# Mamba block and two attention layers on one core: one order for the whole run per engine, set-up split between engines, silu as one ScalarE function, two more PSUM banks for the last attention tiles

## What is computed

```python
# mamba
u = x @ in_w + in_b
u = silu(conv4(u) + conv_b)                      # causal, 4 taps, per channel
delta = softplus((u @ dt1_w + dt1_b) @ dt2_w + dt2_b)
A_bar = exp(delta[..., None] * A)                # 16 states per channel
h = A_bar * h + Bu                               # a scan over 256 tokens, per state
y = (einsum(h, C) + D_vec * u) * silu(x @ gate_w + gate_b)
x = layernorm(x + y @ out_w + out_b)
# twice, with weights of its own each time
h = shift_token(x);  q, k, v = split(h @ wqkv)   # 8 heads of 64
q, k = rotary(l2norm(q) * qs, l2norm(k) * ksc)
x = x + local_attention(q, k, v) @ wo            # windows of 64, own and previous
h = layernorm(shift_token(x)) * lg + lb
a, g = split(h @ w1 + b1);  x = x + (a * gelu(g)) @ w2 + b2
# end: layernorm(mamba's output + the layers' output)
```

## Time and profile before

| What | us |
|---|---|
| median of 3 runs | 1185.32 |
| lowest and highest of them | 1182.23, 1191.19 |
| the profiled execution | 1198.52 |
| its span, first to last instruction | 1196.7 |

### The profile page before, as it was taken

The page is one execution under the profiler, slowest core; times in us unless marked ns, Lnnn a source line. Parts: engine busy times, 40 slices in busy tenths (PEclk is TensorE's granted clock), DMA queues, the critical chain, the costliest instruction groups (busy, mean ns, idle before and its releaser), DMA issues. The chain is left out here.

```text
span 1196.7 us, 26584 instructions
## 1 busy us (share of the span) xinstructions
PE 981.6 (82%) x10304; PEld 575.6 (48%) x10304; DVE 964.0 (81%) x1758; ACT 815.7 (68%) x1833; POOL 480.4 (40%) x261
## 2 busy tenths in 40 slices
PE   2557778888998999899999989898989788876664
PEld 0013344445564556455555655464646465553452
DVE  6595888899889989999999999999999575624612
ACT  1533874786799689886888698869895657642631
POOL 0002420654356525644454545545455344303401
PEclk9587789899999999999999999999999889978967
DMA  6000000000000010001000010000010001000100
GB/s 211 7 1 14 14 11 14 10 20 15 24 10 19 15 28 15 24 19 29 15 23 15 9 38 24 15 24 15 15 24 6 15 24 24 15 10 4 24 10 10
DMA packets 22001, 25.54 MB, mean 21 GB/s; under 512 B 2614, under 2 KB 13937, under 8 KB 21873
## 3 DMA queue, kind: packets, MB, share of 16 engines
q1 hardware_dynamic: 21873, 23.82, 7.8%
HBM read 9.13 MB, written 2.10 MB: 9 GB/s over the span
## 5 line engine op out<-in xcount | busy, mean ns | idle before, releaser
L505 POOL TENSOR_TENSOR rn<-ssc,expo 128x16 f32<-128x16 f32 x64 | 213.2, 3332 | 399.6 <-DVE ssc L863 389.5
L646 ACT ACTIVATE prob<-BB,nbias,rn 128x128 f32<-128x128 f32 x512 | 226.5, 462 | 99.7 <-DVE nbias L905 98.8
L803 DVE TENSOR_TENSOR_SCAN scan<-du,decay 128x1028 f32<-128x1028 f32 x128 | 288.8, 2288 | 2.4 <-ACT decay L591 1.8
L591 ACT ACTIVATE decay<-delta,negA 128x1024 f32<-128x1024 f32 x128 | 145.0, 1159 | 14.9 <-DVE scan L803 14.3
L999 PE MATMUL Y<-scan,diag 64*64 64x512 f32 x1024 | 143.4, 639 | 13.5 <-DVE scan L803 13.5
L999 PE MATMUL A<-wqkv,hT 128*128 128x512 f32 x256 | 131.2, 637 | 9.6 <-DVE ks L880 8.7
L511 POOL TENSOR_TENSOR kr<-kc,ks 128x512 f32<-128x512 f32 x64 | 115.1, 1798 | 26.5 <-DVE ks L880 24.6
L859 DVE TENSOR_REDUCE ss<-sq 128x16 f32<-128x1024 f32 x64 | 77.5, 1211 | 50.6 <-ACT sq L609 50.5
L900 DVE TENSOR_REDUCE nmax<-BB 128x4 f32<-128x512 f32 x128 | 81.8, 680 | 31.9 <-PE BB L999 31.2
L646 ACT ACTIVATION_READ_ACCUMULATOR prob<-BB,nbias,rn 128x1 f32 x512 | 106.8, 209 | 0.0
L609 ACT ACTIVATE sq<-A 128x512 f32<-128x512 f32 x128 | 72.0, 610 | 31.2 <-PE A L999 31.0
(11 more groups left out here) (146 smaller groups left out, 2014.6 us busy)
## 6 DMA issues: line engine op xcount, KB each, us to landing
v_even<-v_odd SPq DMA_DIRECT2D x96, 128.0 KB, 2.3
xT<-in_xT SPq DMA_DIRECT2D x8, 256.0 KB, 2.7
x<-in_x SPq DMA_DIRECT2D x8, 256.0 KB, 3.8
out<-outb SPq DMA_DIRECT2D x8, 256.0 KB, 2.5
wqkv<-in_wqkv SPq DMA_DIRECT2D x1, 1536.0 KB
w<-in_w SPq DMA_DIRECT2D x1, 682.0 KB
wo<-in_wo SPq DMA_DIRECT2D x1, 512.0 KB
bv<-in_bv SPq DMA_DIRECT2D x1, 328.0 KB
```

The source lines that it names most:

```text
L505: pool.tensor_tensor(rn[:, q % 2, :], ssc[:, :], expo[:, 0:2 * HEADS], ALU.pow).then_inc(rn_sb, 1)
L591: act.activation(decay[:, at % A_RING, :, 1:], delta[:, :, :], ACT.Exp, scale=negA[:, n:n + 1]).then_inc(decay_sb, 1)
L646: ins = act.activation(prob[:, h, :], B[a][:, c * P:(c + 1) * P], ACT.Exp, bias=nbias[:, q % 2, h:h + 1], scale=rn[:, q % 2, h:h + 1], acc ...
L803: dve.tensor_tensor_scan(state, step, a, 0.0, ALU.add, ALU.mult).then_inc(scan_sb, 1)
```

## The change

- Each engine's order is now a written list for the whole run (`PE_ORDER` and so on). Nothing repeats. QUAD and TILE are the same, and in the middle of the run each scan block starts after the same or nearly the same number of tiles as before.
- The first three weight transfers (in_w, pv, gate_w) have a semaphore of their own. PE and ACT wait for it alone at the start. xT comes as rows of one array. DVE convolves group 0 before it makes the coefficients.
- GpSimd makes the small identity, the 34 diagonal matrices and the scaled rotary tables. The mask is made by DVE inside the first `sums`.
- Silu is ACT's Silu function, from the convolution's output to u, and from PSUM to the gate. The two tanh instructions' products on DVE are gone; of DVE's step the difference of neighbouring u stays (`differences`).
- `row_max` multiplies all eight maxima by rn in one instruction; `softmax` waits once for it.
- For tiles 53, 55, 57, 59, 61 and 63 (`LATE`) the banks Y0 and Y1, as a pair `YY`, take BB's place.
- SIZES allows groups of other sizes; all are 2 as before.

The core of the diff:

```diff
-TURNS = GROUPS + 17
...
+LATE = [q for q in range(FIRST[-4], len(TILE)) if q % 2]
...
+def banks_of(step, args):
+    banks = HOLDS.get(step, "")
+    return "Y" if banks == "B" and args[0] in LATE else banks
...
-        Y = [bank(f"Y{i}") for i in range(HALF)]
+        YY = ctx.enter_context(nc.psum_tensor("YY", [P, 2 * TOK], F32))
+        Y = [YY[:, i * TOK:(i + 1) * TOK] for i in range(HALF)]
...
+        def pair(q):
+
+            return YY if q in LATE else BB
...
+            for dst, src in [(in_w[:, :], t["in_w"]), (pv[:, :], t["pv"]), (gate_w[:, :], t["gate_w"])]:
+                sp.dma_start(dst, src).then_inc(w_first, 16)
...
+            pool.wait_ge(coeff_done, 1)
+            for h in range(HALF):
+                for n in range(0, NST + 1):
+                    ins = pool.tensor_scalar(diag[:, h, n, :], ident64[:, :], wsum[:, h, n:n + 1], None, ALU.mult)
+            ins.then_inc(diag_done, 1)
...
-            act.wait_ge(w_mamba, M_W)
-            act.activation(negA[:, :], bv[:, BV["A_log"]:BV["A_log"] + NST], ACT.Exp).then_inc(a_exp, 1)
-            act.wait_ge(setup_done, 1)
+            act.wait_ge(w_first, F_W)
...
+            def silu_u(g):
+                act.wait_ge(conv, HALF * TAPS * (g + 1))
+                if g:
+                    act.wait_ge(y_ps, 2 * HALF * g)
+                    act.wait_ge(du_sb, g)
+                act.activation(u[:, both(g), 1:], hu[:, both(g), :], ACT.Silu).then_inc(u_sb, 1)
...
-            def tanh_u(g):
-                act.wait_ge(conv, HALF * TAPS * (g + 1))
...
-                for a in range(2):
-                    dve.wait_ge(max_sb, 2 * q + a + 1)
-                    dve.tensor_tensor(nbias[:, q % 2, a::2], nmax[:, a::2], rn[:, q % 2, a:HEADS:2],
-                                      ALU.mult).then_inc(nmax_sb, 1)
+                dve.wait_ge(max_sb, 2 * q + 2)
+                dve.tensor_tensor(nbias[:, q % 2, :], nmax[:, q % 2, :], rn[:, q % 2, 0:HEADS], ALU.mult).then_inc(nmax_sb, 1)
...
+            convolve(0, 0)
+            convolve(0, 1)
+            coefficients()
...
-            pe.wait_ge(w_mamba, M_W)
-            pe.wait_ge(setup_done, 1)
-            pe.wait_ge(zeros_ready, 1)
+            pe.wait_ge(w_first, F_W)
...
+                if q == LATE[0]:
+                    pe.wait_ge(m_sum, GROUPS)
```

More of the change, by code:

```diff
@@ L134 @@
[L134 to L137, removed]
-def order(table):
-    for turn in range(TURNS):
-        for step, age, *rest in table:
-            g = turn - age
-            if not 0 <= g < GROUPS:
-                continue
-            if step in TILE_STEPS:
-                yield step, (TILE.index((rest[0], g, rest[1])),) + tuple(rest[2:])
-            elif step in FFN_STEPS:
-                yield step, (QUAD.index((rest[0], g)),) + tuple(rest[1:])
-            elif step == "layer_T":
-                yield step, (rest[0], g)
-            else:
-                yield step, (g,) + tuple(rest)
@@ L158, with tiles_of, tok_of, rows_of @@
-ORDER = {"PE": list(order(PE_TURN)), "ACT": list(order(ACT_TURN)), "DVE": list(order(DVE_TURN)),
-         "POOL": list(order(POOL_TURN)), "SP": list(order(SP_TURN))}
+def tiles_of(g):
+    return SIZES[g] * SEQ // P
+def tok_of(g):
+    return SIZES[g] * SEQ
+def rows_of(g):
+    lo = sum(SIZES[:g]) * SEQ
+    return slice(lo, lo + tok_of(g))
+QUAD = [(l, turn - l) for turn in range(GROUPS + LAYERS - 1) for l in range(LAYERS) if 0 <= turn - l < GROUPS]
+TILE = [(l, g, i) for l, g in QUAD for i in range(tiles_of(g))]
@@ new lines, with order @@
+v_even 46, v_even 47, v_even 48, v_even 49, v_even 50, v_even 51, v_even 52, store 4, v_even 53, v_even 54,
+v_even 55, v_even 56, v_even 57, v_even 58, v_even 59, v_even 60, v_even 61, v_even 62, store 5, v_even 63,
+store 6, store 7"""
+def order(text):
+    steps = [word.split() for word in text.split(",")]
+    return [(step, tuple(int(n) for n in numbers)) for step, *numbers in steps]
+ORDER = {"PE": order(PE_ORDER), "ACT": order(ACT_ORDER), "DVE": order(DVE_ORDER), "POOL": order(POOL_ORDER), "SP": order(SP_ORDER)}
@@ L170, in _held @@
     for step, args in ORDER["PE"]:
-        held[step, args] = [last[b] for b in HOLDS.get(step, "") if b in last and last[b] != (OWN.get(step), args)]
-        for b in HOLDS.get(step, ""):
+        banks = banks_of(step, args)
+        held[step, args] = [last[b] for b in banks if b in last and last[b] != (OWN.get(step), args)]
+        for b in banks:
             last[b] = step, args
@@ L344, in build @@
         v_sb = signal("v_sb")
-        ve_sb = [signal(f"ve_sb{i}") for i in range(TILES)]
+        ve_sb = [signal(f"ve_sb{i}") for i in range(V_RING)]
         ss_sb = signal("ss_sb")
@@ L590, in decays @@
                     act.wait_ge(scan_sb, at - A_RING + 1)
-                act.activation(decay[:, at % A_RING, :, 1:], delta[:, :, :], ACT.Exp,
+                act.activation(decay[:, at % A_RING, both(g), 1:], delta[:, both(g), :], ACT.Exp,
                                scale=negA[:, n:n + 1]).then_inc(decay_sb, 1)
@@ L1232, in down @@
                 free("down", f)
-                for i in range(TILES):
+                for i in range(tiles_of(g)):
                     for c, (lo, n) in enumerate(CH):
```

677 lines of the change are left out of this document (430 added, 247 removed).

## The result

The changed kernel takes 1128.3 us (median of four runs, 1122.4 to 1129.6) against 1188.3 for the kernel before on the same chip (1182.2 to 1196.3): a ratio of 0.9485, 95% interval 0.9426 to 0.9545. Measured once more with the experiments it took 1125.5, ratio 0.9455 (0.9423 to 0.9487). The forecast was 1116 us, a ratio of 0.942 to the median of the runs shown. So the direction, the size and the range (1085 to 1148) held. Several terms of the sum did not, and their errors went both ways. That the sum is near is in good part luck, and this is what the rest is about.

A forecast was written before the change was run, and what follows sets the result against it. The prediction took DVE to bound the middle, PE close behind, with chains at start and end. Gains of 17.8 + 25 + 5 + 10 + 11 = 68.8 us, subtracted from the median, gave 1116 us, range 1085 to 1148.

The forecast's parts named there:

- Start: Up to the first scan: shorter chain moves it from 51.19 to 33.4, gaining 17.8 us; between 9 lost and 18 gained.
- rival of late matrices: At the start: GpSimd finishes the diagonal matrices 27 us late at the upper price, giving 1143 us; chance 0.05.
- Early stretches: Two stretches before 300.6 us, attention not yet full: 5 us gained for both, between 0 and 11.4.
- Middle: Five full periods: VectorE loses 5.7 us of work per group, gaining 5.0 per period, 25 us; between 0 and 49.
- So DVE bounds the middle: Full periods: DVE, busy 119.8 of 125.8 us or 119.1 of 123.2, sets their length, with PE close behind.
- I give them nothing either way: Written order lists, nearly the old ones in the middle: no gain or loss counted for them.
- 95% or more: Sign to look for in the full periods of about 119 us: PE's busy share at 95% or more.
- Table loads: ScalarE: ten more loads, 1.28 us each with nothing behind; 4.3 us net if uncovered. Rival with drain: 1130 us, chance 0.02.
- Drain: From 921.2 to 1057 us: free banks for odd tiles save waits, gaining 10 us; between 0 and 25.
- Last four tiles: Softmax of tiles 60 to 63: second bank pair cuts 11.7 to 8.0 us per tile, gaining 11; between 0 and 15.
- The middle does not move: Rival for the full periods: PE's order and waits are the bound, DVE's saving becomes idle time; 1141 us, chance 0.2.
- The written order packs better: Rival: DVE's own idle time goes too, 24 us more, and 6 in the drain; 1086 us, chance 0.2.

The follow-up runs named there:

- after_again: The changed kernel as it is, measured again beside follow-up runs: 1125.48 us, ratio 0.9455 to the kernel before.
- after: The changed kernel in its first measurement and profile, against the kernel before: 1128.3 us, ratio 0.9485.
- turns: The changed kernel driven by the five old repeated order tables, keeping the new banks, GpSimd set-up, Silu and single nbias: 1191.35 us, ratio 1.0015 to the kernel before.
- dve_back: The changed kernel with two unused products per group and a second nbias product per tile put back on VectorE: 1138.46 us, ratio 0.9577 to the kernel before.
- dve_less: The changed kernel with VectorE summing squares over only 32 of a head's 64 channels: 1119.38 us, ratio 0.9397 to the kernel before.
- no_mask: The changed kernel without PE's products that write the mask ahead of the scores: 1115.71 us, ratio 0.9392 to the kernel before.
- tanh_for_silu: The changed kernel with Tanh in place of Silu, 48 table loads instead of 58: 1120.01 us, ratio 0.9407 to the kernel before.
- one_bank: The changed kernel with BB alone for late tiles, transposes moved behind the previous tile's probabilities where needed: 1167.34 us, ratio 0.9820 to the kernel before.
- old_then_new: The changed kernel following the old order tables until the last group's mamba, then the written lists: 1155.10 us, ratio 0.9722 to the kernel before.
- setup_dve_warm: The changed kernel with diagonal matrices and rotary tables back on VectorE and two early table loads on ScalarE: 1116.47 us, ratio 0.9386 to the kernel before.

## Why the prediction was right or wrong

**Start: 17.8 forecast, 11.3 measured.** The shape was right: the first product waits only for gate_w, the convolution starts at once, the coefficients run behind it. Three terms were mis-sized. (1) gate_w is there at 6.04, not 5.3, +0.7. (2) I counted one more table load on the chain, and there are two others: upre's at 9.93, no longer hidden since ACT has nothing before it to do, and decay's at 33.74, where delta to scan took 3.91 instead of 2.58. The convolution started half a us before both upre were done, which gave a little back. The first scan was thus at 36.29, not 33.4. In after_again it was at 34.32, by PE's clock, so these 2.9 are those of one execution. (3) The diagonal matrices on POOL took 0.44 each, not 0.3 (15.1 us from 21.59, end 36.7, not 32.1). In after that alone would have delayed PE, not the scans, which started at 36.29. What I hadn't priced is what POOL does to DVE beside it: from the first scan to the end of the first mamba it is 45.9 us (48.8 in after_again), and 42.2 with POOL idle. "GpSimd had nothing else to do" was no cover, since its work takes DVE's time. 17.8 less 2.9 less 3.6 is the measured 11.3. The rival of late matrices, at 0.05, is in fact what after_again shows, and DVE's wait for PE behind it was 4.96 us, far under its 27.

**Early stretches: 5 forecast, 10.1 measured**, inside the bound of 11.4. turns, without the new lists, gains 1.6 there. So most of this is the order too.

**Middle: 25 forecast, 13.9 measured, and not for the reason given.** The step that failed is "So DVE bounds the middle". It rested on a busy share of 96%. But the same new operations in the old order run periods of 126.1, slower than before by 2.0 with 3.5 us less on DVE. dve_back's first four periods are as those of after; dve_less takes about 3 us away and gets 0.8. The second failed step is "I give them nothing either way" for the lists. With the new operations they carry all of the middle's gain: without them it is a loss of 2.0 per period. The two errors went opposite ways, and the sum came out half right by luck. PE is at 93 to 95% of a period, near the forecast of "95% or more", but no_mask shows it isn't the bound either. The nbias of 385 ns, of which I had called most waiting, is a matter of the order too: one takes 0.17 us unless it meets GpSimd's operations on k (see turns).

**Table loads: right for one, too low for the ten.** 58 instead of 48, 1.28 us each, and the next instruction follows within 0.01 us (30.00 and 31.29 in the timeline of after). The Trainium skill's drain of 1380 ns (page ScalarE: Activation LUTs, section "What ACT_TABLE_LOAD costs") would give 2.66 us between the two, and it isn't there. Ten loads cost 5 to 8 us by medians (tanh_for_silu), where I had 4.3 for the balance of ScalarE if nothing covered it, and counted nothing in the sum.

**Drain: 10 forecast, 25.3 measured**, just past the bound of 25. From the last add to softmax 59 PE was busy 113.3 of 138.7 us before and 102.5 of 113.4 after. That it would fill up was right (90%): its idle time fell by 14.5, near the 16 of which I had taken two thirds. The other 10.8 is PE's busy time itself, a term that the sum did not have: the granted clock rose from 0.91 to 0.98 in that stretch. And the gain needs both the banks and a list that puts the next tile's transposes ahead of prob: neither turns nor one_bank has any of it.

**Last four tiles: 11 forecast, 11.9 measured.** 7.7 us per tile against a forecast of 8.0, through the mechanism named: in the chain of after, only qkT, the scores, nmax and nbias stand between two softmaxes. The stretch from softmax 59 to 60 gained 4.4, where I had nothing; turns gains 2.3 there. The cause is open.

**The rivals.** "The middle does not move" came half true, as my own case did (13.9 lies between its 0 and my 25), and was wrong on PE. "The written order packs better" was right in kind: the order gained in the middle, the early stretches and the drain, though without taking DVE's idle time as I had put it.

**The sum.** Against the stages the forecast was 6.5 too high at the start and 11.1 in the middle, and 5.1, 15.3, 4.4 and 0.9 too low in the others; the rest lost 0.7. These nearly cancel. A total of 68.8 against 76.1 by spans, or 60.0 by medians, says little for the terms.

**What stays open.** Which steps of which list make up the chain that holds a period. Lists of before on some engines with new ones on others were not run, only the cut in time (old_then_new). ScalarE, busy 102 of 122 us, was relieved of its table loads alone, and GpSimd, busy 58 to 60, of nothing in the middle.

## What to carry to other kernels

On engines with fixed orders, a busy share of 95% doesn't say that the engine is the bound: take 3 us away from it in a test before you forecast a gain, and price the order itself, which may be worth more than every operation changed. More buffers may pay only if the order makes use of them, so test the two together and each alone. Before handing small set-up work to GpSimd, see whether VectorE runs long two-input instructions at that time; an idle engine isn't free to use if its instructions and the busy one's keep each other out.

## What the hardware showed that I had not expected

- GpSimd's 128x128 product took 0.45 us with VectorE waiting and 2.39 to 2.44 beside its scans; a diagonal matrix took 0.44 and up to 2.5. The scan, 2.27 alone, took up to 4.26. The slowdown is both ways.
- GpSimd's 128x64 tensor_scalar took 0.44 us alone, VectorE's 0.25 (34 in 15.1 and, in setup_dve_warm, in 5.62).
- One small DVE instruction, nbias of 8 elements, took 0.48 us on average in the old order (turns) and 0.19 in the new (after). Beside GpSimd's operations on k single ones took up to 0.94.
- The same products of PE took 8 us less in the drain when PE was idle for 10 us there (old_then_new, granted clock 0.99) than when it was idle for 26 (turns, 0.93).
